# A gated feed-forward whose intermediate h is turned by VectorE squares and SBUF-to-SBUF transfers instead of TensorE transposes

## The chip, the cores and the metric

One core of one Trainium2 chip runs the whole program. The metric is the device time of one execution in microseconds (us); several executions are timed and their median is compared.

## What is computed

Two feed-forward layers with a layer norm behind each, on 2048 tokens of 1024 features. The change touches the first one only.

```python
s = silu(x @ w_gate.T)                 # 2048 x 2752
s[the 1376 smallest |s| of each row] = 0
h = s * (x @ w_up.T)
x = layernorm(x + h @ w_down.T)
x = layernorm(x + qlora_ffn(x))        # second feed-forward, low-rank terms added
```

Everything is float32. Products are taken with float32r operands, each split into a high and a low part, so that one product is three matmuls: high by high, low by high, high by low.

## The kernel before, in words

**Blocks and chunks.** The 2048 tokens are worked in NB = 4 blocks of TB = 512 tokens, four tiles t of 128. The 2752 columns of h are cut into NJ = 6 chunks j: four of 512, one of 384, one of 320. `SETS[j]` names the 128-row pieces c of h that a chunk fills: 4, 4, 4, 4, 3 and 3 of them (22, the last of them with 64 valid rows). TensorE computes gate chunk by chunk (`gate`, `gate_1` for block 1), then the down product of the block before (`down(b - 1)`, 44 pieces), then up of its own block (`up`). Block 0 does gate and up first. The whole order is written out by hand; each engine has its own program and waits on counters.

**Weight pieces.** One step of TensorE is a piece: a 128-row slice of a weight against four token tiles, 12 matmuls. A gate or up chunk is 8 pieces. The pieces pass through a ring of RING = 5 slots (`wh`, `wl`). SyncE (SP) issues the load of piece n into its slot when TensorE has used piece n - 5 (`load`, L355 to L360, a wait on `pe_used`). ScalarE (ACT) casts it to the high part (L621), GpSimd (POOL) subtracts to get the low part (L514), and only then may TensorE use it. Every one of these queues works strictly in the order written. In the first 8 pieces of a gate an x tile (`x_in_place`, `xTh`, `xTl`) travels beside each weight piece.

**Turning h.** The down product needs h with its 2752 columns on the partitions. h stands with tokens on the partitions, in `v` (block 0: in `w0`). VectorE (DVE) multiplies the up product into it (L1115, counter `u_freed`), which also frees that PSUM bank. `turn` on TensorE (L1352 to L1366) then transposes each 128x128 part against an identity into freed banks, inside the next chunk, behind its piece 3 (block 0: inside `gate_1`). ACT copies the banks to `hTh` (L685) and DVE subtracts to get `hTl` (L1132). Between products DVE masks the next chunk (`masked`, L1099 and L1102). `t_done`, `t_hi` and `t_lo` count these steps; TensorE waits for `t_lo` before a bank is used again.

**Search.** For each block DVE and ACT search the threshold of the mask (L921, L668 and their helpers) while TensorE does the down product of the block before. `take_down` on DVE, behind the search, frees the banks that `up` begins with.

**Space.** `s0` and `w0` of block 0 lie over `hTh` and `hTl`; `y` lies over `hTh` from piece YC = 14 on, so `D_ORDER`, the order in which down takes the pieces of h, begins with pieces 14 and up. x1 of the block before leaves `y` through ACT's DMA queue.

Of the kernel before, what the change touches and what calls it, by code (L numbers as in the profile page):

```python
# [25 lines left out]
P = 128  # L26
# [13 lines left out]
TAIL = I - (NC - 1) * P  # L40
RING = 5
# [15 lines left out]
D_ORDER = SETS[NJ - 2][::-1] + list(range(SETS[NJ - 2][0] - 1, YC - 1, -1)) + SETS[NJ - 1][::-1] + list(range(YC - 1, -1, -1))  # L57
# [98 lines left out]
def program(nc, xT, xtok, wg, wu, wd, w13, w2, a13, a2, b1, b3, b2, out):  # L156
    x1 = nc.dram_tensor("x1", (NB, P, NT, H), F32, kind="Internal").ap()
    with ExitStack() as ctx:  # L158
# [24 lines left out]

        s0 = sb("s0", [P, NT * I], F32, 4, offset=at["hTh"])
# [128 lines left out]
        t_done, t_hi, t_lo = sem("t_done"), sem("t_hi"), sem("t_lo")  # L313
# [40 lines left out]
        def _(sp):  # L354
# [56 lines left out]
            def load_small():  # L411

                sp.wait_ge(t_done, NC * NB)
# [201 lines left out]
        def _(act):  # L615
# [33 lines left out]
            def gate(b):  # L649

                for j in range(NJ):
                    for i in range(KH):
# [5 lines left out]
                        if b >= 2 and j == 0 and i == KH - 1:  # L658
                            turned(b - 1, NJ - 1, 1)
# [84 lines left out]
            def gate_1():  # L744
                for j in range(NJ):
                    for i in range(KH):
# [7 lines left out]
                        if 1 <= j <= NJ - 2 and i == 5:  # L754
                            turned(0, j - 1, (j - 1) % 2)
                        if j == NJ - 1 and i == 1:
                            turned(0, NJ - 2, 1)
                        if j == NJ - 1 and i == 5:
                            turned(0, NJ - 1, 0)

            def down_then_up(b):
# [3 lines left out]
                evac(b, NJ - 1)  # L765
                ahead = iter(range(3, ND))
# [11 lines left out]
            for d in range(ND):  # L778
                high_d(NB - 1, d)
                if d == 2:  # L780
                    turned(NB - 1, NJ - 1, 1)
# [5 lines left out]
                if d >= ND - NW2 - 2 and d < ND - 2:  # L787
                    e = d - (ND - NW2 - 2)
                    if e == 0:
                        act.wait_ge(t_done, NC * NB)  # L790
# [89 lines left out]
        def _(dve):  # L880
# [223 lines left out]
            def take_up(b):  # L1104

                masked(b, 0)
                for j in range(NJ):
                    for t in range(NT):
# [6 lines left out]
                        V.tensor_tensor(s, banks[2 * t + j % 2][:, 0:width(j)], s, ALU.mult).then_inc(u_freed, 1)  # L1115
                    if j < NJ - 1:
# [3 lines left out]
                    turned(b, j, j % 2)  # L1120

            def turned(b, j, p):

                if b == 0:
                    dve.wait_ge(t_done, SETS[j][-1] + 1)
                if b == 0 and j == NJ - 1:
                    step(V.memset(hTl[TAIL:P, NC - 1, :].bitcast(F32), 0.0))
                    st.done()
                for m, c in enumerate(SETS[j]):
                    rows = P if c < NC - 1 else TAIL  # L1130
                    dve.wait_ge(t_hi, NC * b + c + 1)
                    V.tensor_tensor(hTl[0:rows, c, :], banks[2 * m + p][0:rows, :],  # L1132
                                    hTh[0:rows, c, :].bitcast(F32), ALU.subtract).then_inc(t_lo, 1)
# [15 lines left out]
            mask_w0(0)  # L1149
            for j in range(NJ - 2):  # L1150
                take_gate(1, j)
                turned(0, j, j % 2)
                mask_w0(j + 1)
            mask_w0(NJ - 1)
            turned(0, NJ - 2, 1)
            take_gate(1, NJ - 2)
            turned(0, NJ - 1, 0)
            take_gate(1, NJ - 1)
            for b in range(1, NB):
# [11 lines left out]
            dve.wait_ge(t_done, NC * NB)  # L1171
# [150 lines left out]
        def _(pe):  # L1322
# [8 lines left out]
            def chunk(b, base, j, done, first_waits, inside=None, takes_x=False):  # L1331


                for i in range(KH):
# [14 lines left out]
                    if inside is not None:  # L1349
                        inside(i)  # L1350

            def turn(b, j, p):  # L1352

                pe.wait_ge(u_freed, 8 + 4 * NJ * b + 4 * (j + 1))
                pe.sem_inc(passed_pe, 1)
                for m, c in enumerate(SETS[j]):
                    for t in range(NT):

                        for first, rows in ((c * P, P),) if c < NC - 1 else ((I - P, P), (c * P, TAIL)):
                            if b == 0:  # L1360
                                o = in_chunk(j, t).start + first - FIRST[j]
                                h = w0[:, o:o + rows]
                            else:
# [326 lines left out]
```

## Time and profile before

| | |
|---|---|
| three runs | 1955.87, 1956.67 (median), 1958.53 us |
| the profiled execution, its own time | 1959.35 us |
| its span, first to last instruction | 1957.6 us |
| TensorE busy | 1929.8 us, 99% |
| VectorE, GpSimd, ScalarE busy | 1235.9, 912.9, 730.3 us |
| mean granted TensorE clock | 0.997 |

The span is the stretch between the first and the last instruction of the profiled execution; 1.75 us of its time lie around it. A matmul's busy time is modelled and overlaps the next one's, so the pace of TensorE is read from the distance of two starts.

### The profile page before, as it was taken

What the parts mean: (1) busy time and instruction counts of PE and PEld (TensorE: products, weight loads), DVE (VectorE), ACT (ScalarE), POOL (GpSimd) and SP (SyncE); (2) the same over time, 40 slices, a digit from 0 to 9 for tenths busy, and PEclk for the clock granted to TensorE, in tenths of its full rate; (3) what the DMA queues carried; (4) which work ended last, traced back from release to release, by engine and by line L of the source; (5) the groups of instructions that cost most, each with busy time, mean ns of one, the idle gap of its engine ahead of it and who ended that gap; (6) DMA issues with size and microseconds to landing.
All of it is one profiled execution on the core that took longest, in us unless ns stands there. A gap on an engine that the chain in (4) does not pass through costs nothing. (4 is left out here: it accounts for less than half of the span.)

```text
span 1957.6 us, 24665 instructions
## 1 busy us (share of the span) xinstructions
PE 1929.8 (99%) x9320; PEld 1618.5 (83%) x9320; DVE 1235.9 (63%) x1823; ACT 730.3 (37%) x1184; POOL 912.9 (47%) x705
## 2 busy tenths in 40 slices
PE   9999999999999999999999999999999999999998
PEld 8897978988789888888988988789788777887776
DVE  2147975689864326897632489865016999469963
ACT  4356444463233336523243463233242332123312
POOL 5446884445545544554464445444473332013310
PEclk9999999999999999999999999999999999999999
DMA  4333333334344333434243334333543132212212
GB/s 145 92 103 92 114 108 86 92 98 140 88 131 132 95 87 106 140 96 134 82 140 94 99 97 140 93 126 90 171 155 103 44 116 100 71 60 72 101 44 86
DMA packets 102114, 203.67 MB, mean 104 GB/s; under 512 B 11492, under 2 KB 27876, under 8 KB 100688
## 3 DMA queue, kind: packets, MB, share of 16 engines
q1 hardware_dynamic: 97384, 185.28, 31.0%
q10 hardware_dynamic: 4608, 16.78, 2.1%
q8 instruction: 74, 1.21, 0.3%
q14 instruction: 48, 0.39, 0.1%
HBM read 185.24 MB, written 16.78 MB: 103 GB/s over the span
## 5 line engine op out<-in xcount | busy, mean ns | idle before, releaser
L514 POOL TENSOR_TENSOR wl<-w_in_place,wh 128x512 fp32r<-128x512 f32 (+2 forms) x552 | 712.9, 1295 | 666.3 <-ACT wh L621 666.0
L621 ACT CAST wh<-w_in_place 128x512 fp32r<-128x512 f32 (+2 forms) x560 | 328.1, 589 | 772.5 <-DMA w_in_place<-in_wu 301.3
L1327 PE MATMUL banks<-wh,xTh 128*128 128x512 f32 (+2 forms) x1536 | 567.6, 370 | 9.7 <-POOL wl L514 5.7
L1329 PE MATMUL banks<-wh,xTl 128*128 128x512 f32 (+2 forms) x1536 | 564.7, 368 | 0.0
L1328 PE MATMUL banks<-wl,xTh 128*128 128x512 f32 (+2 forms) x1536 | 564.5, 368 | 0.0
L1327 PEld LDWEIGHTS banks<-wh,xTh 128*128 128x128 f32 x1536 | 289.1, 188 | 53.5 <-POOL wl L514 8.6
L1329 PEld LDWEIGHTS banks<-wh,xTl 128*128 128x128 f32 x1536 | 289.0, 188 | 40.4
L1328 PEld LDWEIGHTS banks<-wl,xTh 128*128 128x128 f32 x1536 | 289.3, 188 | 39.6
L1327 PE MATMUL banks<-wh,hTh 128*128 128x512 f32 x672 | 263.3, 392 | 4.5 <-POOL wl L514 4.5
L1329 PE MATMUL banks<-wh,hTl 128*128 128x512 f32 x672 | 262.3, 390 | 0.0
L1328 PE MATMUL banks<-wl,hTh 128*128 128x512 f32 x672 | 262.1, 390 | 0.0
L907 DVE TENSOR_SCALAR sgn<-v 128x512 int8<-128x512 f32 (+2 forms) x72 | 54.8, 762 | 186.5 <-ACT v L647 186.5
L668 ACT ACTIVATE junka<-v,negt 128x1376 int8<-128x1376 f32 x96 | 138.3, 1441 | 82.5 <-DVE negt L915 82.5
L1327 PEld LDWEIGHTS banks<-wh,hTh 128*128 128x128 f32 x672 | 126.6, 188 | 34.1 <-POOL wl L514 8.3
L1329 PEld LDWEIGHTS banks<-wh,hTl 128*128 128x128 f32 x672 | 126.5, 188 | 26.5
L921 DVE TENSOR_SCALAR_CACHE_REDUCE junkd<-v,tc 128x2752 int8<-128x2752 f32 x48 | 147.6, 3076 | 0.9
L1328 PEld LDWEIGHTS banks<-wl,hTh 128*128 128x128 f32 x672 | 126.5, 188 | 26.1
L1252 DVE SCALAR_TENSOR_TENSOR acc<-h,a2raw,acc 128x512 f32<-128x512 f32 (+1 forms) x168 | 146.4, 912 | 1.6
L1327 PE MATMUL banks<-xsh,w13h 128*128 128x512 f32 (+1 forms) x352 | 142.5, 405 | 0.0
L1328 PE MATMUL banks<-xsl,w13h 128*128 128x512 f32 (+1 forms) x352 | 137.6, 391 | 0.0
L1329 PE MATMUL banks<-xsh,w13l 128*128 128x512 f32 (+1 forms) x352 | 137.4, 390 | 0.0
L514 POOL TENSOR_TENSOR w13l<-w_in_place,w13h 128x512 fp32r<-128x512 f32 x44 | 65.6, 1510 | 107.8 <-ACT w13h L802 107.7
(144 smaller groups left out, 2176.4 us busy)
## 6 DMA issues: line engine op xcount, KB each, us to landing
w_in_place<-in_wd SPq DMA_DIRECT2D x176, 256.0 KB, 2.6
w_in_place<-in_wg SPq DMA_DIRECT2D x128, 256.0 KB, 2.6
w_in_place<-in_wu SPq DMA_DIRECT2D x128, 256.0 KB, 2.6
w_in_place<-in_w SPq DMA_DIRECT2D x54, 256.0 KB, 2.9
x_in_place<-in_xT SPq DMA_DIRECT2D x32, 256.0 KB, 3.8
y<-in_xtok SPq DMA_DIRECT2D x4, 2048.0 KB, 8.0
x<-y ACTq DMA_DIRECT2D x16, 512.0 KB, 4.2
xa<-x SPq DMA_DIRECT2D x16, 512.0 KB, 4.2
```

The source lines that it names most:

```text
L514: nc.gpsimd.tensor_tensor(lo, landed, hi.bitcast(F32), ALU.subtract).then_inc(done, 1)
L621: nc.scalar.copy(hi, piece).then_inc(hi_done, 1)
L668: ins = nc.scalar.activation(junka[:, :], v[:, t, h * (I // 2):(h + 1) * (I // 2)], ACT.Sign, bias=negt[:, t:t + 1], accum_out=ssum[:, t - ...
L907: step(V.tensor_scalar(sgn[:, t, cols(j)], s, 0.0, 2.0, ALU.is_ge, ALU.mult))
L921: step(V.tensor_scalar(junkd[:, :], v[:, t, :], tc[:, 0, t:t + 1], None, ALU.is_lt, ALU.add, accum_out=tc[:, 1, t:t + 1]))
L1252: step(V.scalar_tensor_tensor(out=part, in0=h2[0:rows, i, :], scalar=w, in1=part, op0=ALU.mult, op1=ALU.add))
L1327: nc.tensor.matmul(dst, ah, bh, start=start, stop=False)
L1328: nc.tensor.matmul(dst, ah, bl, start=False, stop=False)
L1329: return nc.tensor.matmul(dst, al, bh, start=False, stop=stop)
```

## The change

Behind each product chunk, DVE transposes h in 32x32 squares from `v` (or `w0`) into a new buffer `squares`, which lies over `hTh` (`turn`, now on DVE: one STREAM_TRANSPOSE for each token tile, and two more for the tail piece). A square is then turned in itself, but stands in the partition group of its tokens. SP moves the groups: `send_squares` issues 8 SBUF-to-SBUF DMAs in each of two halves, 16 for a chunk, each from 32 partitions to 32 partitions, into `landed`, which lies over `hTl`. ACT copies `landed` to `hTh` (over the squares), DVE subtracts into `hTl` in place. There are 384 such DMAs: 4 blocks, 6 chunks, 16 each.

TensorE's `turn` and its 368 transposes go. It waits for `u_freed` where banks are used again, and for `t_lo` of the piece it takes in `down`. `D_ORDER` begins with pieces 15 and 14, then chunk 4's, then chunk 5's. The tokens of a tile are permuted on the host (`xtok`, and the output back) so that the groups come out in place. For block 0 the sends stand in the gate of block 1, for the others two chunks behind in `up`, and for the last two chunks of a block in the next gate (or, in the last block, in its `down`).

```diff
-D_ORDER = SETS[NJ - 2][::-1] + list(range(SETS[NJ - 2][0] - 1, YC - 1, -1)) + SETS[NJ - 1][::-1] + list(range(YC - 1, -1, -1))
+D_ORDER = list(range(SETS[NJ - 2][0] - 1, YC - 1, -1)) + SETS[NJ - 2][::-1] + SETS[NJ - 1][::-1] + list(range(YC - 1, -1, -1))
...
+            def send_squares(b, j, half):
+
+                c = slice(SETS[j][0], SETS[j][-1] + 1)
+                sp.wait_ge(squares_done, NT * (NJ * b + j + 1))
+                sp.sem_inc(passed_sp, 1)
+                for g in range(2 * half, 2 * half + 2):
+                    for a in range(GROUPS):
+                        sp.dma_start(landed[SQ * a:SQ * (a + 1), c, g * P:(g + 1) * P],
+                                     squares[SQ * g:SQ * (g + 1), c, a, :]).then_inc(t_in[j % 2], 16)
...
             def load_gate(b):
                 for i in range(NG):
                     load_gu(wg, gate_at(b), i)
+                    j = i // KH
+                    if b == 1 and j and i % KH in (5, 6):
+                        send_squares(0, j - 1, i % KH - 5)
+                    if b == 1 and i >= NG - 1:
+                        send_squares(0, NJ - 1, 0)
+                    if b >= 2 and i in (0, 1):
+                        send_squares(b - 1, NJ - 2, i)
+                    if b >= 2 and i in (KH, KH + 1):
+                        send_squares(b - 1, NJ - 1, i - KH)
...
             def load_up(b):
                 for i in range(NG):
                     load_gu(wu, up_at(b), i)
+                    j = i // KH
+                    if b and j >= 2 and i % KH < 2:
+                        send_squares(b, j - 2, i % KH)
...
                     load_d(b - 1, d)
+                    if b == 1 and d == 0:
+                        send_squares(0, NJ - 1, 1)
...
             for d in range(ND):
                 load_d(NB - 1, d)
+                if d in (0, 1):
+                    send_squares(NB - 1, NJ - 2, d)
+                if d in (3, 4):
+                    send_squares(NB - 1, NJ - 1, d - 3)
...
-            def turned(b, j, p):
+            def turned(b, j):
 
-                for m, c in enumerate(SETS[j]):
-                    act.wait_ge(t_done, NC * b + c + 1)
-                    if c == YC and b:
-                        act.wait_ge(x1_out, 16 * NT * b)
-                    nc.scalar.copy(hTh[:, c, :], banks[2 * m + p][:, :]).then_inc(t_hi, 1)
+                act.wait_ge(t_in[j % 2], 16 * GROUPS * GROUPS * (NJ // 2 * b + j // 2 + 1))
+                for c in SETS[j]:
+                    nc.scalar.copy(hTh[:, c, :], landed[:, c, :]).then_inc(t_hi, 1)
...
-                        if i == KH - 1 and j:
-                            turned(b, j - 1, (j - 1) % 2)
+                        if i == 1 and j >= 2:
+                            turned(b, j - 2)
...
                 evac(b, NJ - 1)
+                if b == 1:
+                    turned(0, NJ - 1)
...
+                    turn(b, j)
                     if j < NJ - 1:
                         masked(b, j + 1)
                     if j == 0:
                         norm_bias(b - 1)
-                    turned(b, j, j % 2)
+                    turned(b, j)
+
+            def turn(b, j):
+
+                if b and j == SETS_Y:
+                    dve.wait_ge(x1_out, 16 * NT * b)
+                    dve.sem_inc(passed_dve, 1)
+                for t in range(NT):
+                    dve.wait_ge(u_freed, 8 + 4 * NJ * b + 4 * j + t + 1)
+                    src = w0[:, in_chunk(j, t)] if b == 0 else v[:, t, cols(j)]
+                    full, tt = width(j) // P, slice(SQ * t, SQ * (t + 1))
+                    c = SETS[j][0]
+                    ins = V.transpose(squares[:, c:c + full, :, tt],
+                                      src[:, 0:full * P].rearrange("p (c a u) -> p c a u", a=GROUPS, u=SQ))
...
+                    ins.then_inc(squares_done, 1)
...
                 for j in range(NJ):
-                    if j >= 2:
-                        turned(b, j - 2)
-                    chunk(b, up_at(b), j, u_done, lambda t: waits(j, t), lambda i: inside(j, i))
+                    chunk(b, up_at(b), j, u_done, lambda t: waits(j, t))
...
                     pe.wait_ge(lo_done, down_at(b) + d + 1)
+                    if n == 0:
+                        pe.wait_ge(t_lo, NC * b + c + 1)
+                        pe.sem_inc(passed_pe, 1)
...
-            turn(NB - 1, NJ - 1, 1)
-            down(NB - 1, lambda t, n: turned(NB - 1, NJ - 2 + n))
+            down(NB - 1, lambda t, n: taken_up(NB - 1, 4 * (NJ - 2 + n) + t + 1))
```

SP's queue, from the end of block 1's gate into its down product (`w_in_place` is a weight piece, in_wg gate, in_wd down). Before, and behind it the change:

```order
L360 DMA w_in_place<-in_wg 128x384 x8
L360 DMA w_in_place<-in_wg 128x320 x8
L360 DMA w_in_place<-in_wd 128x512 x29
```

```order
L366 DMA w_in_place<-in_wg 128x384
L366 DMA w_in_place<-in_wg 128x320 x6
L384 DMA landed<-squares 32x3x128 x8
L366 DMA w_in_place<-in_wg 128x320
L384 DMA landed<-squares 32x3x128 x8
L366 DMA w_in_place<-in_wg 128x320
L384 DMA landed<-squares 32x3x128 x8
L366 DMA w_in_place<-in_wd 128x512
L384 DMA landed<-squares 32x3x128 x8
```

32 sends stand between four weight pieces that followed each other directly. Next, SP's queue where up of block 1 ends and the gate of block 2 begins, with the change (before, the L384 rows are not there):

```order
L366 DMA w_in_place<-in_wu 128x320
L384 DMA landed<-squares 32x4x128 x8
L366 DMA w_in_place<-in_wu 128x320
L384 DMA landed<-squares 32x4x128 x8
L366 DMA w_in_place<-in_wu 128x320 x4
L375 DMA x_in_place<-in_xT 128x512
L366 DMA w_in_place<-in_wu 128x320
L375 DMA x_in_place<-in_xT 128x512
L366 DMA w_in_place<-in_wu 128x320
L375 DMA x_in_place<-in_xT 128x512
L366 DMA w_in_place<-in_wg 128x512
L384 DMA landed<-squares 32x3x128 x8
```

Each half of a chunk stands behind one weight load and ahead of the next. Last, DVE's queue in up of block 1, chunk 0: the end of it before, and then the start and the end of it with the change.

```order
L1115 TENSOR_TENSOR v<-banks,v 128x512 x4
L1099 SCALAR_TENSOR_TENSOR v<-v,tc 128x512
```

```order
L1145 TENSOR_TENSOR v<-banks,v 128x512 x4
L1163 STREAM_TRANSPOSE squares<-v 128x16x32 x4
L1129 SCALAR_TENSOR_TENSOR v<-v,tc 128x512
```

```order
L1121 SCALAR_TENSOR_TENSOR nbias<-mv,rstd 128x4
L1178 TENSOR_TENSOR hTl<-landed,hTh 128x512 x4
L1145 TENSOR_TENSOR v<-banks,v 128x512 x4
L1163 STREAM_TRANSPOSE squares<-v 128x16x32 x4
```

Four transposes stand between the product and the masks, and the subtraction of a chunk still stands ahead of the next chunk's product.

## Rows read from the trace of the kernel before

**Rows 1.** Part 1 of the page, TensorE (busy us, share, instructions)

```profile
PE 1929.8 (99%) x9320; PEld 1618.5 (83%) x9320; DVE 1235.9 (63%) x1823; ACT 730.3 (37%) x1184; POOL 912.9 (47%) x705
```

**Rows 2.** Waits of TensorE (us in total, times, longest us)

```profile
PE banks L1327 <- POOL wl L514: 10.2, 14, 3.2
```

**Rows 3.** Groups by line, TensorE, the transposes (busy us, mean ns of one | idle)

```profile
L1365 PE MATMUL banks<-ident,v 128*128 128x128 f32 (+1 forms) x276 | 33.1, 272 | 0.7 <-DVE v L1115 0.7
L1365 PE MATMUL banks<-ident,w 128*128 128x128 f32 x92 | 11.0, 272 | 0.0
```

**Rows 4.** Timeline (start us, us, what), TensorE around one turn

```profile
533.45 1.91 PE L1365 MATMUL banks<-ident,v 128*128 128x128 f32 x16
535.11 0.48 PE L1327 MATMUL banks<-wh,xTh 128*128 128x512 f32 x1
535.42 0.39 PE L1328 MATMUL banks<-wl,xTh 128*128 128x512 f32 x1
535.65 0.40 PE L1329 MATMUL banks<-wh,xTl 128*128 128x512 f32 x1
```

**Rows 5.** Timeline, TensorE, neighbouring starts at widths 384 and 320

```profile
593.71 0.35 PE L1327 MATMUL banks<-wh,xTh 128*128 128x384 f32 x1
593.89 0.34 PE L1328 MATMUL banks<-wl,xTh 128*128 128x384 f32 x1
...
1354.70 0.31 PE L1329 MATMUL banks<-wh,xTl 128*128 128x320 f32 x1
1354.85 0.31 PE L1327 MATMUL banks<-wh,xTh 128*128 128x320 f32 x1
```

**Rows 6.** Timeline, SP's DMA issues in the last down product

```profile
1374.44 0.33 SPq L360 DMA_DIRECT2D w_in_place<-in_wd  x1
1374.82 0.43 SPq L414 DMA_DIRECT2D a13s<-in_a  x1
1375.29 0.42 SPq L415 DMA_DIRECT2D a2raw<-in_a  x1
1385.69 1.20 SPq L422 DMA_DIRECT2D braw<-in_b  x4
```

**Rows 7.** DMA issues (count, KB each, median us from issue to landing)

```profile
w_in_place<-in_wd SPq DMA_DIRECT2D x176, 256.0 KB, 2.6
w_in_place<-in_wg SPq DMA_DIRECT2D x32, 160.0 KB, 2.2
```

**Rows 8.** Timeline, one piece on ACT and POOL, and POOL at width 320

```profile
1398.21 0.62 ACT L621 CAST wh<-w_in_place 128x512 fp32r<-128x512 f32 x1 [9.27 <-DMA w_in_place<-in_wd]
...
1398.90 2.58 POOL L514 TENSOR_TENSOR wl<-w_in_place,wh 128x512 fp32r<-128x512 f32 x2 [8.53 <-ACT wh L621]
...
618.55 0.86 POOL L514 TENSOR_TENSOR wl<-w_in_place,wh 128x320 fp32r<-128x320 f32 x1 [1.10 <-ACT wh L621]
```

**Rows 9.** Timeline, DVE: a mask, four products, four masks of block 0

```profile
531.66 1.67 DVE L1102 SCALAR_TENSOR_TENSOR v<-sgn,v 128x512 f32<-128x512 int8 x1
544.33 2.73 DVE L1115 TENSOR_TENSOR v<-banks,v 128x512 f32<-128x512 f32 x4 [7.06 <-PE banks L1329]
...
304.85 3.18 DVE L1140 SCALAR_TENSOR_TENSOR w<-v,tc,w 128x512 f32<-128x512 f32 x4
```

**Rows 10.** Timeline, TensorE behind a gap at an up's start; windows, PEclk the granted clock

```profile
499.06 0.47 PE L1327 MATMUL banks<-wh,xTh 128*128 128x512 f32 x1 [1.98 <-issue]
501.21 0.63 PE L1328 MATMUL banks<-wl,xTh 128*128 128x512 f32 x1
501.63 0.63 PE L1329 MATMUL banks<-wh,xTl 128*128 128x512 f32 x1
...
501.00:503.00 2.00, 2.00 (x6) 1.52 (x6) 2.00 (x4) 0.00 (x0) 0.77 (x1) 0.50 0.03 8
```

**Rows 11.** Timeline, TensorE behind 18 small DMAs in SP's queue

```profile
1400.22 0.50 PE L1327 MATMUL banks<-wh,hTh 128*128 128x512 f32 x1 [3.21 <-POOL wl L514]
```

**Rows 12.** Part 3 of the page, SP's queue (packets, MB, share of 16 engines)

```profile
q1 hardware_dynamic: 97384, 185.28, 31.0%
```

More of the change, by code:

```diff
@@ L56 @@
 YC = NC - Y_ROWS
-D_ORDER = SETS[NJ - 2][::-1] + list(range(SETS[NJ - 2][0] - 1, YC - 1, -1)) + SETS[NJ - 1][::-1] + list(range(YC - 1, -1, -1))
+SETS_Y = next(j for j in range(NJ) if SETS[j][-1] >= YC)
+D_ORDER = list(range(SETS[NJ - 2][0] - 1, YC - 1, -1)) + SETS[NJ - 2][::-1] + SETS[NJ - 1][::-1] + list(range(YC - 1, -1, -1))
 assert TAIL == P // 2 and sorted(D_ORDER) == list(range(NC))
@@ L180, in program @@
         hTl = sb("hTl", [P, NC, TB], F32R, 4)
+        squares = sb("squares", [P, NC, GROUPS, P], F32, 4, offset=at["hTh"])
+        landed = sb("landed", [P, NC, TB], F32, 4, offset=at["hTl"])
         s0 = sb("s0", [P, NT * I], F32, 4, offset=at["hTh"])
@@ L312, in program @@
         u_done, u_freed = sem("u_done"), sem("u_freed")
-        t_done, t_hi, t_lo = sem("t_done"), sem("t_hi"), sem("t_lo")
+        squares_done, t_hi, t_lo = sem("squares_done"), sem("t_hi"), sem("t_lo")
+        t_in = [sem(f"t_in{i}") for i in range(2)]
         d_done, d_evac = sem("d_done"), sem("d_evac")
@@ L753, in gate_1 @@
                             copy_u(NJ - 1)
[L754 to L759, printed above, removed]
+                        if j and i == KH - 1:
+                            turned(0, j - 1)
             def down_then_up(b):
@@ L1119, in take_up, with turned @@
                         norm_bias(b - 1)
-                    turned(b, j, j % 2)
[L1122 to L1130, printed above, removed]
+                    turned(b, j)
[10 more added lines that the diff above has]
+                                      src[:, 0:full * P].rearrange("p (c a u) -> p c a u", a=GROUPS, u=SQ))
+                    if width(j) % P:
+                        step(ins)
+                        for a in range(0, GROUPS, 2):
+                            ins = V.transpose(squares[:, NC - 1, a:a + 2, tt],
+                                              src[:, full * P:width(j)].rearrange("p (a u) -> p a u", u=SQ))
+                            if not a:
+                                step(ins)
+                    ins.then_inc(squares_done, 1)
+            def turned(b, j):
+                for c in SETS[j]:
                     dve.wait_ge(t_hi, NC * b + c + 1)
-                    V.tensor_tensor(hTl[0:rows, c, :], banks[2 * m + p][0:rows, :],
-                                    hTh[0:rows, c, :].bitcast(F32), ALU.subtract).then_inc(t_lo, 1)
+                    V.tensor_tensor(hTl[:, c, :], landed[:, c, :], hTh[:, c, :].bitcast(F32),
+                                    ALU.subtract).then_inc(t_lo, 1)
             def mask_w0(j):
@@ L1149, in _ @@
             mask_w0(0)
+            turn(0, 0)
             for j in range(NJ - 2):
                 take_gate(1, j)
[L1152 removed]
+                turned(0, j)
                 mask_w0(j + 1)
+                turn(0, j + 1)
             mask_w0(NJ - 1)
[L1155 removed]
+            turn(0, NJ - 1)
             take_gate(1, NJ - 2)
[L1157 removed]
+            turned(0, NJ - 2)
             take_gate(1, NJ - 1)
+            turned(0, NJ - 1)
             for b in range(1, NB):
@@ L1329, in three, with chunk @@
                 return nc.tensor.matmul(dst, al, bh, start=False, stop=stop)
-            def chunk(b, base, j, done, first_waits, inside=None, takes_x=False):
+            def chunk(b, base, j, done, first_waits, takes_x=False):
                 for i in range(KH):
@@ L1348, in chunk @@
                     ins.then_inc(pe_used, 1)
[L1349 to L1363, printed above, removed]
-                                h = v[:, t, first:first + rows]
-                            ins = nc.tensor.transpose(banks[2 * m + p][0:rows, t * P:(t + 1) * P], h, ident[:, :])
-                    ins.then_inc(t_done, 1)
-            def turned(b, j):
-                pe.wait_ge(t_lo, NC * b + SETS[j][-1] + 1)
-                pe.sem_inc(passed_pe, 1)
             def silu_taken(b, n):
@@ L1379, in copied, with taken_up, freed @@
                 pe.wait_ge(u0_copied, n)
+            def taken_up(b, n):
+                pe.wait_ge(u_freed, 8 + 4 * NJ * b + n)
+                pe.sem_inc(passed_pe, 1)
             def gate(b):
-                def inside(i):
-                    if i == 3:
-                        turn(b - 1, NJ - 1, 1)
+                def freed(j, t):
+                    if b and j < 2:
+                        taken_up(b - 1, 4 * (NJ - 2 + j) + t + 1)
+                    pe.wait_ge(g_freed, 4 * NJ * b + 4 * j + t + 1)
                 for j in range(NJ):
-                    if b and j < 2:
-                        turned(b - 1, NJ - 2 + j)
-                    chunk(b, gate_at(b), j, g_done, lambda t: pe.wait_ge(g_freed, 4 * NJ * b + 4 * j + t + 1),
-                          inside if b and j == 0 else None, j == 0)
+                    chunk(b, gate_at(b), j, g_done, lambda t: freed(j, t), j == 0)
             def gate_1():
@@ L1688 @@
     r = run(nc, [arrays], core_ids=[0])
-    return np.ascontiguousarray(r.results[0]["out_y"].transpose(0, 2, 1, 3)).reshape(2, 1024, 1024)
+    y = r.results[0]["out_y"].reshape(NB, NT, SQ, GROUPS, H).transpose(0, 1, 3, 2, 4)
+    return np.ascontiguousarray(y).reshape(2, 1024, 1024)
```

36 lines of the change are left out of this document (12 added, 24 removed).

## The prediction

> **What bounds the kernel now.** I read part 1 of the page first: TensorE is busy 99% of the span [rows 1], so a microsecond taken from it is a microsecond of the result as long as nothing new makes it wait. Its waits come next: only 10.2 us for weight pieces [rows 2]. So the question is not whether the transposes cost time, but whether the feed of the pieces, which hardly ever is late now, survives what the change puts into the queues. Third I read the timelines of TensorE, SP, ACT, POOL and DVE around one chunk, to get the price of each link of that feed.
>
> The feed: a piece of width 512 is 12 matmuls 0.23 us apart [rows 4], 2.72 us; at width 384 it is 12 x 0.18 = 2.1 us, at 320 12 x 0.15 = 1.8 us [rows 5]. SP may issue piece n when piece n - 5 is used, so it is wanted four pieces later: 10.9, 8.6 or 7.0 us. On that way lie landing (2.6 us, 2.2 us at width 320) [rows 7], the cast (0.6, some 0.4 at 320) and POOL's subtraction (1.3 or 0.9) [rows 8]. What is left is the lateness that SP may have: 6.3 us in wide chunks, 3.5 us in the last one.
>
> **What the change takes away.** From the first transpose of a group of 16 to the next matmul pass 1.66 us, and that matmul holds the engine 0.31 us in place of 0.23 [rows 4]: 1.74 us for 16, 0.109 us each. There are 276 + 92 = 368 [rows 3], so **40 us** go. (Their busy time, 33.1 + 11.0 = 44 us, is the upper end; the overlap with neighbours speaks for the lower.) All of it lies on TensorE, which bounds.
>
> **What it adds on SP.** 384 DMAs, which the trace does not show. Bounds for the issue of one: two DMAs of two rows each cost 1.20 / 4 = 0.30 us each; two of 128 rows directly behind each other start 0.47 us apart, also the one that moves only 22 KB [rows 6]. A send has 32 x 4 = 128 pieces of 512 bytes (96 for the short chunks), so I take 0.47 us. A half is then 3.8 us, and a chunk's two halves with the load between them 8 us of SP, across two pieces. Landing of a send: 2.2 us, as the smallest weight load [rows 7].
>
> The Trainium skill, "DMA: Bandwidth & Descriptors" (Issuing engines are not separate DMA queues), says that the time a sequencer takes to initiate a DMA is usually small beside the DMA itself. By that rule SP would not matter and the sum would stay near the 40 us gain; the rows on SP speak against it here, because the sends stand in the one queue that also feeds TensorE.
>
> **What it adds on DVE and ACT.** Four transposes of 128x512: between the single-source rate and the 0.8 us of a two-source pass, 3.18 / 4 [rows 9]; I take 0.7 us, 2.8 us a chunk. The subtraction reads two SBUF operands now; such passes take 0.8 us beside an idle POOL and up to 1.67 us beside a busy one [rows 9]; I take 0.95, 3.8 us a chunk. Products of a chunk take 2.7 us [rows 9]. ACT's copies are 0.52 us each, as a cast that follows another. None of this is on TensorE's path by itself, but it decides when the squares are ready, and SP waits for them with the weight loads behind it.
>
> **Where it fits.** In a wide chunk of `up`, with t = 0 at the end of the piece that frees the first load's slot: halves 0.4 to 4.2 and 4.6 to 8.4, the third load is issued at 8.4 where it could have been at 5.4; it lands at 11.0, ACT is held by the copies of `landed` until 12.3, cast and subtraction end at 14.3, wanted 16.3. No stall. The same holds for chunks 1 to 3 in the gate of block 1 and for chunk 5's sends in the second chunk of a later gate.
>
> **Where it does not.**
> - *Chunk 5 of up* (t = 0 at the end of chunk 3). DVE ends the subtraction of chunk 2 at 3.7, the product at 6.4, the transposes at 9.2; SP is there at 9.0. Halves to 13.0 and 17.2; the third load lands at 19.4; ACT waits for the sends (18.9), copies to 21.0, cast and subtraction to 22.3. Wanted at 20.6: 1.7 us, three times, **5 us**.
> - *Start of the gate, blocks 2 and 3* (same t). Squares of chunk 4 at 27.4, halves to 31.2 and 35.9 with an x load behind each; the third weight piece is issued at 36.3, lands 38.9, behind the x tile it leaves POOL at 42.2. TensorE ended chunk 5 at 32.9 and wants it at 38.8, after 0.5 us at the piece before: 3.9 us, twice, **8 us**.
> - *End of block 1's gate*. 32 sends stand between four narrow pieces. DVE has the squares of chunk 4 at 23.4 (t = 0 at the end of chunk 3). Halves to 27.2, 31.4, 35.6 and 39.8; the pieces behind them are ready at 30.7, 34.9, 40.1 and 44.3, and TensorE loses 2.7, 2.4, 3.4 and 1.5 us: **10 us**.
> - *Start of the last down product*. Its second piece needs the bank of chunk 5, whose product DVE makes only behind the subtraction of chunk 4 (t = 41.0, TensorE there at 35.6: 5.4 us). Then the squares of chunk 5 are ready at 45.3, SP waits for them behind the fourth piece, halves to 49.1 and 53.3; the fifth and sixth pieces are 4.5 and 1.5 us late: **11 us**.
> - *Search of block 1*. ACT takes the last gate chunk only behind three late casts, 7.5 us after TensorE is through, and DVE has three subtractions more ahead of the search, 2.9 us; 4.9 us of it are hidden by the stalls just counted: the up of block 1, which already waits 1.98 us for DVE [rows 10], begins **5.5 us** later.
> - *Clock*. Behind the gap of 1.98 us matmuls start 0.42 us apart, the granted clock is 0.50, which is the 1.2 GHz level [rows 10]; about eight matmuls at 0.43 in place of 0.23 are 1.6 us. Before that gap the engine was busy. Six of the stalls above are in clusters of 2 us or more: **10 us**.
>
> That these sums are of the right kind shows at a place where the kernel already does it: 18 small DMAs in SP's queue, the first four of them in [rows 6], leave TensorE a gap of 3.21 us [rows 11].
>
> **Sum.** 5 + 8 + 10 + 11 + 5.5 + 10 = 49.5 us lost, less 0.7 us that the last turn waited [rows 3]: 49. Against the profiled execution's own 1959.35 us: 1959.35 - 40 + 49 = 1968. The median of the runs is 2.7 us below that execution, so I forecast **1966 us**, 0.5% slower. About 0.2% (4 us) is what a measurement can tell from no change.
>
> **Rivals.**
> - *The sends are cheap* (faster). If an issue costs 0.33 us, as a lone load does [rows 6], a half is 2.6 us. Then chunk 5 of up fits, the gates lose 1.5 us each, the end of block 1's gate 3.5, the last down 9 (its waits are DVE's), the search 2, the clock 5: about 22 us against 40, so 1939 us. For it: that row. Against it: the DMAs that follow another directly show 0.47 between starts. It decides from 0.39 us per send downward. Chance 0.25.
> - *All of it is hidden* (faster). This is the skill's rule above, taken as a mechanism: SP's issues cost nothing and DVE keeps pace. 1957 - 40 = 1917 us. Against it: the order of SP's queue, and TensorE's bank wait in the last down. Chance 0.08.
> - *Costs and gain cancel*: each stall 1 to 2 us shorter than worked out, as with landings of 1.5 us; 1953 to 1961 us. Chance 0.12.
> - *The DMA engines become the bound* (much slower). SP's packets take 0.31 x 16 x 1957.6 / 97384 = 0.10 us each on their engine [rows 12], at 1.9 KB on average. If a 512-byte packet costs the same, a send is 8 packets an engine, 0.8 us, and a half 6.4 us. Then also wide chunks miss by some 3 to 5 us, 13 times (55 us), and the others by 5 us more (45 us): about 2065 us. By bytes alone the packet would be 0.03 us, and SP's issue stays the bound. Chance 0.10, with all between 1995 and there.
> - *The squares don't help*: that TensorE still has its transposes is excluded by the order, which shows none in `up`.
>
> **The numbers.** The forecast with its neighbourhood (1961 to 1995) has 0.45. Slower 0.45 + 0.10 = 0.55, same 0.12, faster 0.33. The range of 8 in 10 goes from 1932 (leaves out the fully hidden case) to 2000 us (leaves out the bound by the DMA engines).
>
> **What will show it.** Right: TensorE has no group of line 1365 and waits some 35 us more for `wl` and for DVE, in clusters of 2 to 5 us at the starts of gates 2 and 3, at the end of block 1's gate, and at the start of the last down; SP's groups of 8 sends last 3.8 us; granted clock of 0.5 for some 3 us behind each. Wrong: sends at 0.33 us or less, a landing far from 2.2 us, DVE subtractions near 0.7 us, or waits of TensorE in wide chunks, where I see none.

## The result: slower by 90 us, and the profile after

| | before | after |
|---|---|---|
| median of the runs | 1957.6 us (1955.87 to 1959.6, 4 runs) | 2047.55 us (2042.1 to 2052.35, 4 runs) |
| ratio, 95% interval | | 1.0458 [1.0429, 1.0488] |
| span of the profiled execution | 1957.6 us | 2040.3 us |
| TensorE busy | 1929.8 us | 1927.7 us |

The kernel is 4.6% slower. The forecast had the sign (1966 us), but not the size: its range ended at 2000 us. Line numbers below are those of the changed kernel: 366 loads a weight piece, 384 sends squares, 381 is SyncE's wait for them, 655 is the cast of a piece, 548 the subtraction on POOL, 717 ScalarE's copy of `landed`, 1163 and 1168 the transposes on VectorE, 1178 its subtraction, 1375 to 1377 the three matmuls.

Part 1 of the page after answers to [rows 1]:

```profile
PE 1927.7 (94%) x8952; PEld 1601.7 (79%) x8952; DVE 1292.5 (63%) x1950; ACT 729.2 (36%) x1184; POOL 919.5 (45%) x705
```

The transposes are gone (9320 - 368 = 8952 instructions) and with them 44.1 us of busy time [rows 3]. Still the busy time fell by 2.1 us only, so the records of the matmuls that are left add up to 42 us more. And TensorE's idle time rose from 27.8 us (1957.6 - 1929.8) to 112.6, by 85. -44 + 42 + 85 = 83 us is the whole difference of the spans. Most of the 42 us is half clock, but not all. The granted clock is 0.50 in 18 stretches of the trace after, 95.6 us together, and TensorE is busy in 76.0 us of them; before there are 3 stretches, 10.2 us, all busy (the end of the program, where the clock falls in both, is left out). Half of the difference, **33 us**, is what half clock costs. Another 5 us is the overlap of the transposes with their neighbours: `four_sends` below, which lacks them too and hardly stalls, is busy 1891.7 us, 38 less than before, and 40 with the little that its clock costs more. The last 4 us were not taken apart. The row of the granted clock in part 2 shows the slices where it fell (it was 9 in every slice before):

```profile
PEclk9999999799998999999989999999899999999999
```

The waits of TensorE, SyncE's queue, and VectorE (us in total, times, longest), which answer to [rows 2]:

```profile
PE banks L1375 <- POOL wl L548: 91.3, 45, 5.3
PE banks L1375 <- DVE v L1145: 6.1, 1, 6.1
...
SPq L381 <- DVE squares L1163: 10.7, 4, 4.2
...
SPq L381 <- DVE squares L1168: 6.8, 1, 6.8
...
DVE hTl L1178 <- ACT hTh L717: 250.8, 23, 18.4
```

TensorE waits 91.3 us for `wl` in place of 10.2. POOL, which is named, is not the cause: it is the last link of the feed, itself fed late. VectorE's 250.8 us in front of its subtractions of line 1178 (23 waits) are no loss of TensorE in themselves, but the next chunk's masks and transposes stand behind that wait, and SyncE waits for their squares with weight loads behind it: 17.5 us in five waits.

The instructions themselves, by line (duration in ns, lowest, median and highest; for DMAs also us from issue to landing):

```profile
L384 SPq DMA_DIRECT2D landed<-squares x384: 585/599/2296, 275.0 to 1451.9; - x192
...
DMA to landing us min/median/max: 1.9/2.0/6.2
```
```profile
L1163 DVE STREAM_TRANSPOSE squares<-v x72: 400/669/705, 551.2 to 1440.8; 128x512 f32<-128x512 f32 x48, 128x384 f32<-128x384 f32 x12, 128x256 f32<-128x256 f32 x12
...
L1178 DVE TENSOR_TENSOR hTl<-landed,hTh x88: 677/685/1780, 290.6 to 1461.2; 128x512 fp32r<-128x512 f32 x88
```

Landing and the transposes came out as assumed (2.0 and 0.67 us against 2.2 and 0.7), the subtraction cheaper (0.69 at the median against 0.95). The send did not: eight of them fill SyncE's queue for 5.1 us, 0.64 us each from start to start, where the sum had 0.47.

How that reaches TensorE in a wide chunk, where no stall was expected. Timeline (start us, us, what) of SyncE, then ScalarE, POOL and TensorE:

```profile
588.70 5.37 SPq L384 DMA_DIRECT2D landed<-squares  x8
594.20 0.52 SPq L366 DMA_DIRECT2D w_in_place<-in_wu  x1
594.83 5.10 SPq L384 DMA_DIRECT2D landed<-squares  x8
600.04 11.84 SPq L366 DMA_DIRECT2D w_in_place<-in_wu  x7
...
601.39 2.18 ACT L717 CAST hTh<-landed 128x512 fp32r<-128x512 f32 x4 [3.66 <-DMA landed<-squares]
603.48 1.14 ACT L655 CAST wh<-w_in_place 128x512 fp32r<-128x512 f32 x2
...
604.17 6.96 POOL L548 TENSOR_TENSOR wl<-w_in_place,wh 128x512 fp32r<-128x512 f32 x5 [5.08 <-ACT wh L655]
...
605.72 0.50 PE L1375 MATMUL banks<-wh,xTh 128*128 128x512 f32 x1 [1.26 <-POOL wl L548]
```

A clump is a half of a chunk's sends, eight DMAs in a row. From the start of the first clump to the load behind the second pass 11.3 us (600.04 - 588.70), where the forecast's chain had 8. That load has landed at some 602.7 (an estimate: 2.7 us is the median of the loads of line 366), its cast waits until ScalarE has made the four copies, and TensorE gets the piece 1.26 us late.

Where TensorE has less work left in the pieces it holds (narrow chunks, sends in closer succession), it is a series of stalls. SyncE's queue and TensorE at the end of block 1's gate (width 384):

```profile
354.58 6.34 SPq L384 DMA_DIRECT2D landed<-squares  x8
361.03 0.52 SPq L366 DMA_DIRECT2D w_in_place<-in_wg  x1
361.67 5.09 SPq L384 DMA_DIRECT2D landed<-squares  x8
366.87 2.44 SPq L366 DMA_DIRECT2D w_in_place<-in_wg  x5
...
361.40 0.33 PE L1376 MATMUL banks<-wl,xTh 128*128 128x384 f32 x1
361.58 0.34 PE L1377 MATMUL banks<-wh,xTl 128*128 128x384 f32 x1
365.21 0.44 PE L1375 MATMUL banks<-wh,xTh 128*128 128x384 f32 x1 [3.29 <-POOL wl L548]
365.49 0.34 PE L1376 MATMUL banks<-wl,xTh 128*128 128x384 f32 x1
...
367.79 0.53 PE L1376 MATMUL banks<-wl,xTh 128*128 128x384 f32 x1
368.11 0.53 PE L1377 MATMUL banks<-wh,xTl 128*128 128x384 f32 x1
370.97 0.69 PE L1375 MATMUL banks<-wh,xTh 128*128 128x384 f32 x1 [2.34 <-POOL wl L548]
```

Each of the two loads that stand behind a clump (361.03 and the first of those from 366.87) costs TensorE one gap. Behind the first gap the matmuls start 0.32 us apart (367.79, 368.11) in place of 0.18 (361.40, 361.58): the 1.2 GHz level, as in [rows 10]. It lasts into the next gap and beyond it.

### The profile page after: what moved, and what is told of

Same layout as the page of the kernel before. It is cut to its first block and busy times, and to the rows that moved or that the text cites. A ratio compares the mean times of both kernels' runs of the same rounds, so it can differ in the third digit from the quotient of the medians.

```text
span 2040.3 us, 24532 instructions
## 1 busy us (share of the span) xinstructions
PE 1927.7 (94%) x8952; PEld 1601.7 (79%) x8952; DVE 1292.5 (63%) x1950; ACT 729.2 (36%) x1184; POOL 919.5 (45%) x705
## 3 DMA queue, kind: packets, MB, share of 16 engines
q1 hardware_dynamic: 148584, 208.38, 33.6%
## 5 line engine op out<-in xcount | busy, mean ns | idle before, releaser
L548 POOL TENSOR_TENSOR wl<-w_in_place,wh 128x512 fp32r<-128x512 f32 (+2 forms) x552 | 720.6, 1314 | 739.3 <-ACT wh L655 738.9
L1375 PE MATMUL banks<-wh,xTh 128*128 128x512 f32 (+2 forms) x1536 | 578.3, 377 | 75.4 <-POOL wl L548 73.5
L1376 PE MATMUL banks<-wl,xTh 128*128 128x512 f32 (+2 forms) x1536 | 573.6, 373 | 0.0
L1377 PE MATMUL banks<-wh,xTl 128*128 128x512 f32 (+2 forms) x1536 | 573.5, 373 | 0.0
L1375 PEld LDWEIGHTS banks<-wh,xTh 128*128 128x128 f32 x1536 | 296.0, 193 | 131.4 <-POOL wl L548 88.3
L1377 PEld LDWEIGHTS banks<-wh,xTl 128*128 128x128 f32 x1536 | 295.7, 192 | 41.3
L1376 PEld LDWEIGHTS banks<-wl,xTh 128*128 128x128 f32 x1536 | 296.0, 193 | 40.0
L1178 DVE TENSOR_TENSOR hTl<-landed,hTh 128x512 fp32r<-128x512 f32 x88 | 63.1, 776 | 250.8 <-ACT hTh L717 250.8
L937 DVE TENSOR_SCALAR sgn<-v 128x512 int8<-128x512 f32 (+2 forms) x72 | 50.6, 702 | 126.4 <-ACT v L681 126.4
```

The costliest lines, as they stand in the source:

```text
L548: nc.gpsimd.tensor_tensor(lo, landed, hi.bitcast(F32), ALU.subtract).then_inc(done, 1)
L937: step(V.tensor_scalar(sgn[:, t, cols(j)], s, 0.0, 2.0, ALU.is_ge, ALU.mult))
L1178: V.tensor_tensor(hTl[:, c, :], landed[:, c, :], hTh[:, c, :].bitcast(F32), ALU.subtract).then_inc(t_lo, 1)
L1375: nc.tensor.matmul(dst, ah, bh, start=start, stop=False)
L1376: nc.tensor.matmul(dst, ah, bl, start=False, stop=False)
L1377: return nc.tensor.matmul(dst, al, bh, start=False, stop=stop)
```

## The experiments

Each ran against the kernel before on the same chip; the ratio is the one to read. Distances in us between two runs below are differences of ratios times 1957.6 us, where nothing else is said.

**1. Price of a send by its number.** Two edits of the changed kernel move the same bytes in a quarter and in twice the number of DMAs. In the first the squares stay in their own partition group, so that h is not what the reference has there:

```diff
-for a in range(GROUPS):
-    sp.dma_start(landed[SQ * a:SQ * (a + 1), c, g * P:(g + 1) * P], squares[SQ * g:SQ * (g + 1), c, a, :])
+sp.dma_start(landed[:, c, g * P:(g + 1) * P], squares[:, c, g, :])
```

> The changed kernel, but the 16 sends of a chunk are 4 (128 partitions each, same bytes, same 512-byte runs); h then lands in its own partition group, so its squares are not moved and the down product takes it unmoved. Theory A (SP's issue time, 0.635 us a DMA, holds up the weight loads behind it): a chunk costs SP 2.5 us instead of 10.2, nearly all waits of TensorE for wl go, 1957.6 - 40 + some 12 = about 1930 us. Theory B (the DMA engines and the many 512-byte packets hold up the loads): packets and bytes are the same, so 2030 to 2050 us. Theory C (DVE's and ACT's longer chain, waits for the squares, copies of landed): also 2030 to 2050 us.

Measured: 1930.1 us, 0.9840 [0.9816, 0.9865], as theory A expected.

> The changed kernel, but each of the 16 sends of a chunk is cut into two (768 DMAs in place of 384, the same bytes). Theory A: if one issue costs 0.635 us whatever it moves, a chunk's sends hold SP for 20 us in place of 10; no chunk has that slack, so most of the additional 24 x 10 us comes through: 2230 to 2300 us. If the price goes with the descriptors (half as many in each), little changes: about 2050. Theory B: the same bytes and packets, 2040 to 2060 us. Theory C: the same.

Measured: 2308.06 us, 1.1767 [1.1737, 1.1797], 8 us above the range of theory A and far from the others. The sends of the one and the other, by line:

```profile
L383 SPq DMA_DIRECT2D landed<-squares x96: 599/623/2443, 275.1 to 1339.9; - x96
```
```profile
L384 SPq DMA_DIRECT2D landed<-squares x768: 577/597/2095, 276.2 to 1721.0; - x192
```

By the medians a send of up to 256 KB holds SyncE 0.62 us and one of up to 32 KB 0.60 us. What counts is their number: 96 leave a gain of 31 us, 384 turn it into a loss of 90, 768 into one of 346 (each time (ratio - 1) x 1957.6). The bytes are the same, so the DMA engines' bandwidth is not the bound. VectorE's transposes and subtractions and ScalarE's copies are in all three kernels, so by themselves they don't cost the 90 us either.

**2. The sends alone, in the kernel before.** 384 DMAs from `ident` into a scratch tile at the places of the sends; nothing else changes, TensorE keeps its transposes, and nobody waits for the landing. The second has one run of 512 bytes per partition where the first has four of 128.

> The kernel before with TensorE's transposes and everything else in place, and 384 additional SBUF-to-SBUF DMAs of the form 32x4x32 (128-byte runs, 16 KB) in SP's queue at the places of the sends; nobody waits for them. Theory A: the loss of the change without its gain: 1957.6 + 90 + 40 = about 2085 us (2070 to 2100), issue 0.6 us each. Theory B: a quarter of the bytes, less: 1980 to 2020. Theory C: nothing waits for squares here, so near 1960 to 1975 us.

Measured: 2010.98 us, 1.0253 [1.0227, 1.0278].

> As the one above, but each DMA is of the form 32x128 (32 runs of 512 bytes in place of 128 runs of 128 bytes). Theory A with a price per DMA: 0.6 us each again and the time of the one above within 1%. Theory A with a price by form or by descriptors: 0.3 to 0.45 us each and 1980 to 2030 us.

Measured: 2006.01 us, 1.0235 [1.0206, 1.0265].

The expectation was missed: the clumps by themselves cost 50 us, not the 130 (90 + 40) that had to be found. The time lies in the range of theory B (a quarter of the bytes); that fewer bytes are why it is 50 is not excluded by this run alone, but experiment 1 moved all the bytes in 96 DMAs and gained. The form of the send makes no difference, 0.60 and 0.59 us a DMA:

```profile
L382 SPq DMA_DIRECT2D extra<-ident x384: 585/601/1877, 276.7 to 1425.8; - x192
```
```profile
L382 SPq DMA_DIRECT2D extra<-ident x384: 507/590/2262, 275.8 to 1416.3; - x192
```

**3. Is it ScalarE's wait?** To the kernel of experiment 2 is added that ScalarE waits for the extra transfers where it waits for the squares in the changed one:

```diff
+def extra_in(b, j):
+    for half in range(2):
+        act.wait_ge(x_sent[half], 16 * 8 * (NJ * b + j + 1))
```

> The kernel before with 384 extra transfers that carry nothing of use (before_plus_3d, 1.0253 of before), and now ScalarE waits, at the places where the changed kernel waits for its squares, until the sixteen extra transfers of that set have landed. SyncE and VectorE wait for nothing new. The changed kernel is still some 75 us slower than before_plus_3d less the 40 us of transposes. Theory A, ScalarE carries it: the wait for the last of a clump of transfers stands in order ahead of the next casts, so each clump delays TensorE twice; then this run is 1.05 to 1.06 of before (2060 to 2080 us), and the waits of TensorE for the cast weights grow from 40 us to some 90. Theory B, the coupling is in the waits for VectorE (SyncE for the squares, 17.5 us in the trace after, and VectorE's order): then this run stays within 0.5% of before_plus_3d (1.020 to 1.031, 2002 to 2023 us).

Measured: 2010.68 us, 1.0258 [1.0219, 1.0297], the same as without the wait. Theory A of this text falls. (Only the wait is tested: the kernel before has its own copies elsewhere, and none was added.)

**4. Is it VectorE's order?**

```diff
 for j in range(NJ - 2):
     take_gate(1, j)
-    turned(0, j)
     mask_w0(j + 1)
     turn(0, j + 1)
+    turned(0, j)
```
and in `take_up` the subtractions of chunk j come one chunk later.

> The changed kernel with VectorE's order alone altered: the masks and transposes of the next chunk go ahead of the subtractions of the chunk before, so that the squares are ready earlier and VectorE no longer stands at a wait for ScalarE's copy with that work behind it. Same transfers at the same places. Theory A (ScalarE's wait behind the clump of transfers): within 0.5% of the changed kernel, 1.040 to 1.051 of before. Theory B (VectorE's order makes the squares late and SyncE waits for them): SyncE's 17.5 us of waits go, and 15 to 35 us with them, 1.028 to 1.038 of before (2017 to 2037 us).

Measured: 2026.77 us, 1.0343 [1.0300, 1.0385]. The waits of SyncE for squares are gone from its list, and 23 us with them. Theory B holds for this part.

**5. Nobody waits for the clumps; then no clumps.** In `clumps_decoupled` ScalarE's copies come most of a chunk later and VectorE's subtractions two. In `spread` the same transfers stand a few behind each weight piece:

```diff
-if b and j >= 2 and i % KH < 2:
-    send_squares(b, j - 2, i % KH)
+if b and 2 <= j < NJ - 1:
+    send_squares(b, 2 * (i - 2 * KH), 2)
```

> The changed kernel with its 384 transfers still in clumps of eight, but nobody stands in wait for them: ScalarE's copies of the squares come most of a chunk later, VectorE's subtractions two chunks later and its masks and transposes earlier, one semaphore for each set. If the price of a clump on SyncE alone is what before_plus_3d showed (49 us) and the transposes of TensorE saved are worth 40 to 44, this is 1.000 to 1.010 of before (1962 to 1982 us). If clumps cost the changed kernel its 130 us by themselves, it stays at 1.035 to 1.05 (2030 to 2060 us).

Measured: 2015.74 us, 1.0306 [1.0255, 1.0357]: between the two ranges, close under the second.

> The kernel clumps_decoupled with the same 384 transfers spread: two behind each weight piece in the up stages and in gates 2 and 3, three in gate 1, four in the last narrow chunk and in the last down stage. Two cost SyncE 1.27 us of a piece's 2.9 to 4.7 us, so that its five pieces ahead of TensorE are never used up. If the price of a transfer is SyncE's issue time and only clumps make it felt: 0.978 to 0.986 of before (1919 to 1935 us), faster than the kernel before by about the 40 us of transposes and with under 20 us of waits for the cast weights. If each transfer costs time wherever it stands (through the DMA engines or the landing): 1.00 or above (1962 us and more).

Measured: 1947.94 us, 0.9945 [0.9925, 0.9965]. Faster than before, so a send costs nothing like its 0.64 us where it doesn't stand in a clump. `clumps_decoupled` and `spread` differ in the places of the sends, and in block 1's gate in those of ScalarE's copies and VectorE's subtractions: 71 us. But it is above the range, and the timeline tells why (SyncE's queue in the last down stage, then TensorE):

```profile
1364.85 0.33 SPq L366 DMA_DIRECT2D w_in_place<-in_wd  x1
1374.11 1.19 SPq L452 DMA_DIRECT2D braw<-in_b  x4
...
1387.70 0.80 PE L1382 MATMUL banks<-wh,hTh 128*128 128x512 f32 x1 [10.86 <-POOL wl L548]
```

SyncE stands for 9 us ahead of `load_b` until VectorE has cleared the buffer, which comes after the postponed subtractions. `clumps_decoupled` has the same gap, of 10.2 us; without it it would be near 2005 us (an estimate).

**6. Were the 40 us ever gained?** `clumps_decoupled` has neither transposes nor waits for squares, and yet stays at the time of experiment 2, which has all its transposes. That suggested that TensorE had made its transposes in time that a clump costs anyway. The test puts 344 idle ones back:

```diff
+def fill(n, p, freed):
+    freed()
+    for m in range(n):
+        for t in range(NT):
+            nc.tensor.transpose(banks[2 * m + p][:, t * P:(t + 1) * P], ident[:, :], ident[:, :])
```

> The changed kernel, and TensorE turns again: 344 transposes of the constant identity into a bank that is free, after the fourth piece of a chunk as in the kernel before (16 in each of the last five chunks of an up stage and of gate 1, 12 in gates 2 and 3), with the wait for that bank; nobody uses them. They are 37 us of TensorE's own time at 0.109 us. Theory C, the transposes filled the time in which a clump makes TensorE wait for a late weight piece, so that the changed kernel never got the 40 us where clumps fall: 0 to 15 us more than the changed kernel (1.045 to 1.054 of before, 2047 to 2063 us). Rival, gain and price simply add up: 35 to 40 us more (1.063 to 1.067, 2082 to 2090 us).

Measured: 2045.53 us, 1.0434 [1.0414, 1.0453]. The changed kernel with 344 transposes more is as fast as without them: 5 us less by the ratios, within the intervals. That is just below the range of theory C and far from the rival's.

> The kernel spread with three places mended at which its trace shows TensorE waiting: the load of the small matrices, which stood at a wait of 8.9 us for VectorE with the weights of the last down stage behind it (10.9 us of TensorE), comes six pieces later; four transfers a piece in the narrow last chunk become two, or three in the last block; in gate 1 the last two chunks get one or two a piece instead of three. Expected 0.981 to 0.988 of before (1925 to 1938 us): 10 us from the first, 2 to 6 from the rest. If it stays at 0.9945, the waits named weren't what cost spread its distance from four_sends (0.984).

Measured: 1933.21 us, 0.9865 [0.9839, 0.9892], in the range expected. Three places were changed at once; the gap of 10.9 us is gone from the trace, and the others were not tested one by one.

> spread_tuned with the same 344 idle transposes as transposes_back. Here no clump makes TensorE wait, so both theories expect them at nearly their full price: 33 to 40 us over spread_tuned (1.000 to 1.006 of before). If this too costs under 15 us, then transposes of TensorE are cheap wherever they stand, and theory C says nothing of clumps.

Measured: 1968.01 us, 1.0028 [1.0016, 1.0039], 32 us over `spread_tuned` by the ratios and 35 by the medians (both ran on one chip). The same transposes, the same busy time in both kernels:

```profile
L1384 PE MATMUL banks<-ident 128*128 128x128 f32 x344 | 41.1, 272 | 0.0
```
```profile
L1399 PE MATMUL banks<-ident 128*128 128x128 f32 x344 | 41.1, 272 | 0.0
```

and the two kernels' waits of TensorE for `wl`, first with clumps, then spread:

```profile
PE banks L1375 <- POOL wl L548: 68.0, 40, 4.6
```
```profile
PE banks L1390 <- POOL wl L552: 17.0, 19, 2.9
```

With clumps TensorE's idle time falls by 24.9 us when the transposes come back (112.6 to 2042.9 - 1955.2 = 87.7), and busy rises by 27.5 us where the transposes are 41.1, 13.6 us less. 41.1 - 13.6 - 24.9 = 2.6 us, the difference of the spans. Of the 13.6 us some 3 are overlap (in the spread pair the busy time rises by 34.9 us, where TensorE's busy time at a granted clock of 0.50 falls from 13.8 to 6.8, so that the work itself is 38), and the rest is half clock: TensorE's busy time at a granted clock of 0.50 falls from 76.0 to 54.9 us, and half of that is 10.5. So theory C holds: about two thirds of the transposes' time come out of idle time, and somewhat under a third out of half clock. The gaps of 0.8 us and more in the wide and the 384 wide chunks of the three up stages, 22 us in the changed kernel, are 6 us with the transposes back. Spread out, the same work costs about its full price: TensorE's idle time there is 39.0 us without the transposes and 39.8 with them.

`spread_tuned` does all of the change's work and beats both kernels: 1.35% faster than before, 5.7% faster than the changed kernel. Its queue, where the changed kernel has clumps of eight:

```profile
575.69 0.33 SPq L366 DMA_DIRECT2D w_in_place<-in_wu  x1
576.12 1.24 SPq L386 DMA_DIRECT2D landed<-squares  x2
578.41 0.33 SPq L366 DMA_DIRECT2D w_in_place<-in_wu  x1
578.84 1.24 SPq L386 DMA_DIRECT2D landed<-squares  x2
```

## Why the prediction was right in sign and wrong in size

The sign was no firm call: the forecast gave "slower" 0.55, and all times above 1995 us, where the result lies, 0.10. The size failed by its losses. Two accounts of them have to be kept apart; their terms must not be mixed.

The first is read from the trace after, in the terms of the forecast. Spans: 83 us = -40 (transposes) + 85 (idle time of TensorE) + 33 (half clock) + 5 (rest). The forecast: +9 = -40 + 39 (stalls of 5, 8, 10, 11 and 5.5, less 0.7) + 10 (clock). So the term of 40 stood, and **the stalls (39 against 85) and the clock (10 against 33) failed**.

The second is by the runs, and asks what each part of the change does when it is added to a kernel; in parts of 1957.6 us. The clumps of sends in the old kernel: +50 (experiment 2). Four times the bytes in each send, the squares on VectorE, its waits and ScalarE's copies: +35 (from 1.0253 to 1.0434); 23 of the 90 go again when VectorE's order alone is changed. Transposes taken away: +5 between `transposes_back` and the changed kernel, nothing within their intervals.

By the steps of the forecast:

- **"What the change takes away", 40 us.** The price was right: 344 transposes are worth 32 to 35 us in the spread kernel, some 0.10 us each. Nor was it wrong to add it to the stalls, because the forecast worked them out for pieces of 12 matmuls alone, a TensorE that has no transposes any more. What it didn't see is that those stalls hold the 40 us again: inside a clump SyncE bounds and not TensorE, and time freed on TensorE is waited away there. "All of it lies on TensorE, which bounds" is true of the kernel before and of the spread one only. The 130 us that experiment 2 looked for came from the same oversight: they take the 40 for a gain that clumps have to outweigh.
- **A send at 0.47 us, a half at 3.8.** Measured 0.64 and 5.1. This is the step that failed first. The bound was taken from two DMAs behind each other [rows 6], but they are loads from memory. The trace before has no send within SBUF, so its rows could not give the price, and 0.47 was no bound on it. The number in sequence is not the reason: two sends behind a load take 1.24 us in `spread_tuned`, also 0.6 each.
- **"No stall in wide chunks".** With halves of 5.1 us the third load comes 11 us behind the start in place of 8, and the chain that the forecast wrote down (landing, ScalarE's copies, cast, subtraction) ends late. Estimated with its own links, but 0.64 us a send and a landing of 2.0: halves end at 5.5 and 11.2, the copies at 14.7, cast and subtraction at 16.6, wanted 16.3. The 2 us of slack are gone by the price of the send alone; the 1.26 us late of the timeline above are that and some more in each link. From TensorE's gaps of 0.8 us or more: 7 us in the first chunks with sends of block 1's gate, and 22 in the chunks 2 to 4 of the three up stages (chunk 4 is 384 wide), where the forecast had 0. These 29 us are the largest part that was missed.
- **Chunk 5 of up**: 5.2, 5.0 and 5.3 us, 16 against 5. Same place, three times the size. **End of block 1's gate**: six gaps, 19 against 10. **Start of gates 2 and 3**: 9 against 8. **Last down**: 6.1 us for the bank of chunk 5, then 4.0 and 1.9, 12 against 11; the bank wait, 5.4 in the forecast, is the 6.1 us behind line 1145. **Search of block 1**: 5.5 were expected, and no such gap is in the trace.
- **Clock, 10 us.** Measured 33 us, an error of 23. There were over 30 gaps of 0.8 us or more and 18 stretches of half clock, not six clusters; and several gaps of 3 to 5 us were followed by more than eight slow matmuls. TensorE's timeline in `transposes_back`, width 320:

```profile
653.03 0.64 PE L1375 MATMUL banks<-wh,xTh 128*128 128x320 f32 x1 [4.19 <-POOL wl L548]
...
658.00 0.47 PE L1375 MATMUL banks<-wh,xTh 128*128 128x320 f32 x1
658.26 0.47 PE L1376 MATMUL banks<-wl,xTh 128*128 128x320 f32 x1
...
658.88 0.31 PE L1376 MATMUL banks<-wl,xTh 128*128 128x320 f32 x1
659.03 0.31 PE L1377 MATMUL banks<-wh,xTl 128*128 128x320 f32 x1
```

  Starts 0.26 us apart in place of 0.15 for 5.5 us behind one gap of 4.19.
- **The rival "DMA engines"** came nearest in time (2065 us) but for a wrong reason: four times fewer DMAs with the same bytes give 0.984. Its premise, 0.10 us for a packet of 512 bytes, does not hold either: SP's queue has 148584 packets at 33.6% after and 97384 at 31.0% before [rows 12], which makes some 0.025 us for each of the 51200 that were added (an estimate from these shares and the spans). Its step "then also wide chunks miss" is what happened, from the issue of the DMAs and not from their packets. The rule of the Trainium skill, "DMA: Bandwidth & Descriptors" (Issuing engines are not separate DMA queues), that the sequencer's time to initiate a DMA is usually small beside the DMA, does not fit here: the queue is held 0.6 us for a send that lands after 2.0, and eight in a row hold it for 5.1. Spread out (`spread_transposes`), what the forecast concluded from it, that SP would not matter, nearly holds: 384 sends and all the rest cost 5 us with 344 of the 368 transposes still there (1.0028), or 8 us with the 24 that are missing.

Open is how the 35 us divide between the bytes of a send, VectorE, ScalarE's copies and the landing: the reorder of VectorE takes back 23 us of the changed kernel's time, the rest was not taken apart. ScalarE's wait for the transfers cost nothing in the kernel before; whether it does in the changed one, together with the copies, is not shown.

## What to carry to other kernels

Price a DMA that is added to a queue by the queue's time for a DMA of its own kind, and look at the longest clump between two loads that somebody needs, not at the total: from `clumps_decoupled` to `spread`, eight in a row against two to four behind each piece, the same 384 transfers differ by 71 us. Where no row shows the kind, write the forecast for a range of prices and say at which price the slack is gone. A saving on the bounding engine and a stall of the same engine may be added only if the stall is worked out for the kernel without the saved work: in a stretch that another queue bounds, what is saved is only waited longer, and here the engine ran at half clock behind many of the waits. When a wait is moved out of the way, list what stands behind it in every queue; here a small load that waits for VectorE left TensorE a gap of over 10 us until it was moved as well.

## What the runs showed of the hardware that was not expected

- A send within SBUF holds SyncE's queue 0.59 to 0.62 us at the median, whatever it moves (16, 32, 64 or 256 KB, runs of 512 bytes or of 128, 32 partitions or 128), also directly behind a load. Other kinds of DMA have other prices in the same queue: a weight load with nothing directly ahead takes 0.33 us, one directly behind another load some 0.37 (0.47 from start to start [rows 6]), one behind eight sends 0.52, and the loads of two rows 0.30 from start to start [rows 6]. Why the sends take longer is not shown.

```profile
L366 SPq DMA_DIRECT2D w_in_place<-in_wu x192: 327/328/1931, 118.1 to 1420.0; - x192
```

- Transfers within SBUF that carry a quarter of the bytes of a weight load land only 0.7 us sooner (up to 64 KB in 2.0 us, up to 256 KB from memory in 2.7 by the medians). With 256 KB within SBUF (`four_sends`) the median is 3.2 us.
- The loss to half clock (33 us) came on top of the added idle time (85 us), and was some 0.4 of it.
